# GpSimd waits for gathered rows once per fourteen gathers instead of once per seven, in a graph layer with 200000 edges

## The reference

```
x_rel = einsum('nd,rdo->rno', layernorm(x), einsum('rb,bdo->rdo', w_comp, weight))
agg   = segment_sum(x_rel[etypes, src] * norm, dst, num_segments=6250)
x     = x + relu(agg + h_bias + layernorm(x) @ loop_weight)
x     = x + experts(layernorm(x))      # 16 experts of 256-512-256, top 2, then a layernorm
```

## Time and profile before

| | before |
|---|---|
| median of 3 runs | 3305.88 us (3302.12 to 3306.97) |
| the profiled execution's own time | 3305.05 us |
| its span, first to last instruction | 3303.3 us |
| mean granted TensorE clock | 0.847 |
| PE busy | 2350.0 us (71%) |
| GpSimd busy | 1813.9 us (55%) |
| VectorE busy | 940.6 us (28%) |
| ScalarE busy | 658.2 us (20%) |

### The profile page before, as it was taken

The page is one execution under the profiler, slowest core; times in us unless marked ns, Lnnn a source line. Parts: engine busy times, 40 slices in busy tenths (PEclk is TensorE's granted clock), DMA queues, the critical chain, the costliest instruction groups (busy, mean ns, idle before and its releaser), DMA issues. The chain is left out here.

```text
span 3303.3 us, 37521 instructions
## 1 busy us (share of the span) xinstructions
PE 2350.0 (71%) x11549; PEld 1960.3 (59%) x11550; DVE 940.6 (28%) x2032; ACT 658.2 (20%) x1539; POOL 1813.9 (55%) x2000
## 2 busy tenths in 40 slices
PE   2489888878778676757756665754744447999987
PEld 1468777666666565545545444543533337999986
DVE  6343232322223212222122121211211235333338
ACT  3232322222112111101110100000100014333336
POOL 0536566565665656666566566665666612555544
PEclk9689999989889888878878777776867779999999
DMA  6243333333333333323333332222322245222236
GB/s 214 85 135 100 104 98 107 95 96 117 96 96 93 113 91 95 96 85 96 104 91 90 89 97 89 86 87 81 92 86 81 83 139 196 70 70 69 69 94 228
DMA packets 146265, 338.61 MB, mean 103 GB/s; under 512 B 36674, under 2 KB 56290, under 8 KB 146051
## 3 DMA queue, kind: packets, MB, share of 16 engines
q0 software_dynamic: 89296, 245.33, 24.9%
q1 hardware_dynamic: 39311, 59.54, 5.2%
q10 hardware_dynamic: 17588, 32.88, 3.0%
HBM read 292.84 MB, written 47.97 MB: 103 GB/s over the span
## 5 line engine op out<-in xcount | busy, mean ns | idle before, releaser
L1060 POOL DMA_INDIRECT rows<-feat,idx x1540 | 1463.0, 950 | 972.6 <-DMA rows<-feat,idx 550.8
L1282 PE MATMUL psW<-rows,S 128*128 x3920 | 1152.4, 463 | 686.2 <-SPq L1016 676.8
L1282 PEld LDWEIGHTS psW<-rows,S 128*128 128x128 f32 x3920 | 919.3, 239 | 915.1 <-issue 729.3
L1147 DVE TENSOR_TENSOR S<-psHere,coefS 128x896 f32<-128x896 f32 x280 | 300.6, 1089 | 1823.6 <-PE psW L1282 1501.0
L1340 ACT COPY z<-psW 128x512 f32<-128x512 f32 x196 | 114.6, 585 | 1827.9 <-PE psW L1282 1294.4
L1237 PE MATMUL psG<-wb,zT 128*128 128x256 f32 (+1 forms) x1600 | 354.0, 379 | 0.5 <-issue 0.5
L1237 PEld LDWEIGHTS psG<-wb,zT 128*128 128x128 f32 (+1 forms) x1600 | 301.0, 188 | 46.6 <-issue 1.2
L1731 PE MATMUL psH<-xT,w1x 128*128 128x128 f32 x1840 | 226.7, 277 | 2.7 <-issue 2.7
L1731 PEld LDWEIGHTS psH<-xT,w1x 128*128 128x128 f32 x1840 | 216.5, 193 | 4.4 <-issue 4.3
L1740 PE MATMUL psO<-w2s,hT 128*128 x912 | 215.7, 379 | 0.0
L1682 POOL DMA_INDIRECT expert_rows<-os,at_rows x114 | 117.3, 1029 | 169.8 <-DVE os L1789 169.8
(11 more groups left out here) (284 smaller groups left out, 1463.7 us busy)
## 6 DMA issues: line engine op xcount, KB each, us to landing
rows<-feat,idx POOLq DMA_INDIRECT x1568
g<-expert_rows SPq DMA_DIRECT2D x24, 512.0 KB, 5.7
w1s<-in_L_ffn_w SPq DMA_DIRECT2D x8, 1024.0 KB, 10.0
w2s<-in_L_ffn_w SPq DMA_DIRECT2D x16, 512.0 KB, 9.8
feat<-rows SPq DMA_DIRECT2D x24, 256.0 KB, 3.0
fts<-feat ACTq DMA_DIRECT2D x24, 256.0 KB
h<-in_x ACTq DMA_DIRECT2D x24, 256.0 KB
y_rows<-y ACTq DMA_DIRECT2D x24, 256.0 KB
```

What stands on the lines that cost most here:

```text
L1060: e.indirect_dma_start(rows[:, at * H:(at + 1) * H], None, d.feat, bass.IndirectOffsetOnAxis(ap=idx[:, q * GB + u:q * GB + u + 1], axis=0) ...
L1147: e.tensor_tensor(S[h][:, :].rearrange("p (s b n) -> p s b n", s=U, b=B), both[:, h * U:(h + 1) * U, :].unsqueeze(2).to_broadcast([P, U, B ...
L1282: last = e.matmul(to[u], S[h][:, u * ZC:(u + 1) * ZC], of[u], start=False, stop=True, skip_group_check=True)
```

## The change

`landed` is called ahead of gather 0 of each group of fourteen only, and there it waits for the same seven gathers as before, those issued last. The call ahead of gather 7 goes.

```
                     for u in range(GB):
                         at = (q * GB + u) % RB
-                        if u % QB == 0:
-                            landed(i, q * GB + u - QB)
+                        if u == 0:
+                            landed(i, q * GB - QB)
                         e.indirect_dma_start(rows[:, at * H:(at + 1) * H], None, d.feat, ...).then_inc(s_row[at // QB], 16)
```

## The result

| | before | after |
|---|---|---|
| median of 17 runs each | 3305.88 us (3302.12 to 3312.54) | 3326.97 us (3310.19 to 3351.83) |
| ratio, with its 95% interval | 1 | 1.0071 (1.0055 to 1.0087) |
| the profiled execution's own time | 3305.05 us | 3335.88 us |
| span | 3303.3 us | 3334.1 us |
| mean granted TensorE clock | 0.847 | 0.836 |

What follows compares the result with a forecast made beforehand. The prediction took GpSimd's issue of gathers as the bound, a fifth of it standing until the queue is empty. From 3305.05 us it took 254.7 for removed waits and added 3 for the start: 3053 us, range 3040 to 3082.

Steps and rivals of the forecast that it cites:

- What bounds the kernel: Whole layer: bound by GpSimd's issue of gathers, a fifth of it standing until the queue is empty.
- What the change removes: Ahead of gather 7: 110 waits go, each worth 2.315 us to GpSimd, together 254.7 us.
- Does the gap fall to 0.30?: Ahead of gather 7: only the usual 0.30 us issue gap stays, as in fourteen gathers of an earlier stage.
- Does the kept wait grow?: Ahead of gather 0: no growth, 0 us of bounds 0 to 2.3 per period; 3 us taken off at the start.
- Can TensorE take rows faster?: TensorE, line 1282: yes; the early part costs nothing, or 27 us if GpSimd can't build up its lead.
- the wait for line 1016: TensorE's wait for landed rows: should fall from 677 to 420 to 450 us.
- The gain is cut at the seams: Rival: TensorE's early bound costs 27 us (3080), or other GpSimd stops 18 us (3071); chance 0.12.
- The wait moves: Rival: the removed stop returns in the kept wait or inside a gather, gaining 0 us (3305); chance 0.04.
- The queue of descriptors overflows: Rival: gathers 7 to 13 each wait for a landing, 3.5 us apart, 1480 us more (4790); chance 0.03.
- The row named as what would be wrong: Sign against the forecast: GpSimd waiting for TensorE more than some microseconds, meaning the ring is full early.

Runs made afterwards that it cites:

- e9: The changed kernel itself, unedited, timed again in a job with complete records: 3019.98 us, 0.9215 of the kernel before.
- e10: The changed kernel with one wait for landing per 28 gathers instead of per fourteen, complete records: 2886.29 us, 0.8808 of the kernel before.
- e16: Repeat of the changed kernel with one wait per 28 gathers, in another job with complete records: 2882.77 us, 0.8806 of the kernel before.
- e13: Repeat of the changed kernel with no waits for landings left, complete records: 2760.84 us, 0.8432 of the kernel before.
- e5: The changed kernel itself, unedited, timed again in a job with complete records: 3025.42 us, 0.9216 of the kernel before.
- e18: The changed kernel with a GpSimd memset pause ahead of gather 7 that awaits no landing, incomplete records: 3249.03 us, 0.9797 of the kernel before.
- e2: The changed kernel with a GpSimd memset pause ahead of gather 7 that awaits no landing, complete records: 3208.59 us, 0.9788 of the kernel before.
- e15: Repeat of the changed kernel with the memset pause ahead of gather 7, complete records: 3204.82 us, 0.9788 of the kernel before.
- e1: The changed kernel with its remaining wait for landings removed too, complete records: 2760.22 us, 0.8423 of the kernel before.
- e17: The changed kernel with no waits for landings left, in a job with incomplete records: 3652.77 us, 1.1032 of the kernel before.
- e7: The changed kernel plus a SyncE load of 128x8 separate single words behind each landing of seven, complete records: 3020.43 us, 0.9223 of the kernel before.

## Why the prediction was wrong

**What bounds the kernel** was right: in the complete jobs the time follows the number of waits alone. Within one job each, it falls from 220 to 110 waits by 258 and 256 us (2.3 us each), from 110 to 55 by 134 (e9 to e10, 2.4 each), and from 55 to none by 122 (e16 to e13, 2.2 each). The term of *What the change removes*, 2.315 us each, is met.

**What the change removes** and its sum came out in e5 and e9: -258 and -256 us where -252 was forecast. e5 has 109 waits of 269.4 us (some 275 forecast), 453.2 us in 1423 issue gaps (455 in 1430), and 2215.7 us from the first to the last gather (2200).

*Does the gap fall to 0.30?* Yes, in both kinds. In the changed kernel on record the gathers of a group follow each other by 1.25 us even in the midst of an episode. *Does the kept wait grow?* It didn't (269.4 / 109 = 2.47 us in e5).

*Can TensorE take rows faster?* is the step that failed. It costed the early part at nothing, because GpSimd would get ahead of a TensorE that works on at its pace, and it took the pace from the earlier trace rows, where GpSimd never issues more than seven without a break. In the jobs with incomplete records TensorE doesn't keep that pace while fourteen are issued. It loses most where it has most to do: ahead of 600 us, where the step had found it to be the bound itself. In the first fifth a period grew from 22.4 to 26.3 us, where 20.0 was forecast. From the first to the last gather it took 2489.2 us instead of the forecast 2200: 289 us in place of this step's 0. The bound of 27 us that I gave for this step supposed that the lead might not be built up, not that TensorE could be held. Against e5 the profile on record is longer by 3334.1 - 3022.9 = 311 us. Of this 273 lie between the first and the last gather (193.7 to 2682.9 against 157.5 to 2373.2) and 36 ahead of the first. Those 36 are no part of why the change lost: the kernel before has them too (its first gather of the layer is at 197.3 us), and so has e18 (197.2 us, against 159.1 and 158.5 in e2 and e15). In the layer itself e18 is as fast as they are, 2398.2 us from the first gather to the last against 2400.9 and 2395.4. With breaks at seven the other kind of job costs the layer nothing.

A smaller miss: in e5 the wait for line 1016 was 534.3 us and not 420 to 450. The steps of line 1282 took 1105.0 us instead of 1152.4, with a granted clock of 1.00 from 300 to 400 us against 0.95, and a step that is done sooner waits longer for its rows; these 47 us are about half of the miss, and the rest I can't place.

**The earlier trace rows was read for one engine only.** It did show that GpSimd can issue fourteen at 1.25 us. But the same stretch of the kernel before shows what the others did. Busy time from 145 to 162 us, and then TensorE's and ScalarE's timelines:

```profile
145.00:162.00 17.00, 3.96 (x51) 2.79 (x50) 1.70 (x3) 0.94 (x3) 12.95 (x14) 0.56 0.38 112
```

```profile
156.31 0.27 PE L818 MATMUL psE<-typ_b,spread 128*128 128x128 bf16 x1 [0.28 <-issue]
157.01 0.26 PE L818 MATMUL psE<-typ_b,spread 128*128 128x128 bf16 x1 [0.44 <-issue]
165.69 0.50 PE L834 MATMUL psC<-wc,hot 128*128 128x64 bf16 x6 [8.41 <-DVE hot L911]
```

```profile
164.78 0.37 ACT L782 COPY coefS<-psC 128x256 f32<-128x256 f32 x1 [12.35 <-remote]
```

Two starts 0.70 us apart, then nothing for eight; VectorE did three instructions in 17 us, and ScalarE stood 12.35 us for something that the record doesn't hold and went on 2.9 us after the last gather had ended (161.91). That is an episode, in the profile that the prediction had in hand. (In e5 the same fourteen gathers go out from 125.07 to 141.34 us, and TensorE does 496 matmuls from 125 to 157 us.) The prediction noted that "those fourteen were in flight with little beside them"; the little was the effect.

The same stage also shows that seven is no fixed number. Ahead of those fourteen GpSimd issues an edge gather and two gathers of rows and then stops, and already there the others are late: it stands six times for TensorE's transposes, and 413 matmuls take 45 us where e5, with no such stop, needs 25 us for 410. GpSimd's wait in the kernel before, the 45 us, and e5's 25 us:

```profile
POOL edge L723 <- PE psT L808: 22.9, 6, 4.4
100.00:145.00 45.00, 28.35 (x413) 24.46 (x414) 23.02 (x57) 18.93 (x56) 18.14 (x20) 0.74 0.23 67
100.00:125.00 25.00, 20.89 (x410) 17.22 (x409) 21.26 (x52) 18.71 (x56) 18.97 (x20) 1.00 0.47 125
```

About 20 of the 40 us by which the layer starts later than in e5 (197.3 against 157.5 us) are lost in this part, with runs of three: the last edge gather goes out at 143.46 us, in e5 at 123.81. TensorE has 16 matmuls to start in each us there (e5, 410 in 25 us) and 5 in the layer (485 in 100 from 300 us on). So how long a run the others bear seems to hang on how many short instructions they have to do; that is argued, no run varies it alone.

**The rivals.** *The gain is cut at the seams* named the early part as the weak place and was right in that, by a price of 27 us where the two kinds of job differ by about 300. *The wait moves* (3305) would have been nearest in time, but by another mechanism: neither the kept wait nor a gather grew. *The queue of descriptors overflows* had the right sign and the right place (gathers 7 to 13), but not the mechanism: its 3.5 us between gathers never came. In e1 1540 gathers without a wait were issued in 1950.2 us, 1.27 us each, and the median gather is 946 to 949 ns in the changed kernel on record, e1, e5, e17 and e18. What was held were the other engines, not GpSimd. The finite descriptor buffer of the Trainium skill (Perfetto Trace Analysis, the section on the DMA instruction of GpSimd), which I had weighed for this rival, has thus shown itself in no run here.

The row named as what would be wrong, GpSimd waiting for TensorE, is what came (306.8 us).

**Shown:** the same kernel goes from 0.92 to 1.00 and 1.01 of the kernel before between jobs; episodes occur in the incomplete jobs only, and in the layer only with runs longer than seven; the loss grows with the run; a memset of 1.8 us after seven prevents it; empty semaphore instructions cost 180 us in one kind and 1229 in the other.

**Ruled out by the traces:** that the transfers are slower in the incomplete jobs, by a load on the memory or the DMA engines from elsewhere. The packets of the gathers' queue took 24.8% of sixteen engines' 3334.1 us on record and 27.8% of their 3022.9 us in e5, which is 827 and 840 us. Behind the rows of each gather come sixteen packets of 4 bytes, which I take for its increments. They are all in every trace, and the last of them comes 2.41 us after the gather's start in the median on record and in e17, and 2.42 us in e5. If I read these packets rightly, the DMA engines sent the increments as promptly in the one kind as in the other.

**Open:** what is jammed. The gathers' own traffic of descriptors and semaphores, and the records that the profiler writes, would both fit instructions served one per 0.70 us; no run separates them. All 17 executions of the changed kernel on record took 3310 to 3352 us, so whatever it is doesn't come and go within a job; whether it is at work where nothing is recorded, no run tells. What puts a job into one kind or the other isn't known: one chip number had both. It could also be that the lost records are a sign of the jam and not its cause.

## What to carry to other kernels

A wait that looks like pure latency on one engine may be what lets the others be served; price its removal by what every engine did in a stretch of the trace that already has the longer run, not by the pace of the engine that is freed. Before trusting such a trace, count whether it holds the semaphore increments that the program must make, and time the change in more than one job: here one edit was worth -256 us or +10 to +21. Where increments are missing, don't trust the names of the waits: of some 200 us of waits for rows in the changed kernel's profile only 50 bore that name. If such a guard is needed, a pause long enough for the rows to land does it and costs less than awaiting a landing (e2 and e15 against the kernel before, and e18 once in the other kind of job).

## What the runs showed of the hardware that was not expected

- In an episode TensorE and VectorE go on by one instruction per 0.70 us, or per a multiple of it, while GpSimd's indirect gathers, 128 rows of 1 KB, keep 1.25 us; it ends some 2.5 us after the run of gathers (2.6 and 2.9 us in the two shown).
- Awaiting the landing of seven gathers costs 2.2 to 2.4 us each time; the landing is 2.8 us after the issue (median of e5).
- Kernels with breaks at every seven gathers differ by about 1% between the two kinds of job (3277 to 3306 us, 3207 to 3249; in the second pair all of it ahead of the layer), with fourteen by 10% (3022 to 3325), with none by 32% (2760 to 3653).
- Some 230000 more packets of single words beside the gathers (e7) cost nothing that could be measured.
